# State-space stage: order of the decays, C times B over 128 partitions, and two moved VectorE steps

## The chip, the cores and the metric

The kernel runs on one core of a Trainium2 chip. The time is the device time of the whole program in microseconds (us), taken over several executions; the profile is one more execution, recorded by the hardware profiler. The core has TensorE (PE; its weight loads are listed as PEld), VectorE (DVE), ScalarE (ACT), GpSimd (POOL) and the queue engine SyncE (SP), which work side by side and wait for one another by semaphores.

## The reference, cut to what matters

`x` has 2 sequences of 2048 tokens with 512 channels, all in float32. Three layers follow one another, each added to `x`: half a gated feed-forward layer (ternary weights, 2048 hidden), a state-space layer, and the same feed-forward layer again. The change is in the state-space layer:

```
z, x, B_toks, C_toks, dt_toks = split(u @ W_in.T)         # 512, 512, 64, 64, 8 columns
x, B, C = silu(causal depthwise conv of 4 taps (x, B, C) + conv_b)
dt = softplus(dt_toks + dt_bias);  dA = exp(dt * -exp(A_log))       # one per head, 8 heads of 64 channels
S = S * dA_t + dt_t * outer(x_t, B_t);   y_t = S @ C_t              # token by token, state 64 x 64 a head
y = (y + D_param * x) * silu(z);   out = y @ W_out.T
```

## The kernel before, in words

The scan is computed in chunks of 128 tokens. Inside a chunk the sum over earlier tokens becomes a masked product: C times B (128 by 128 tokens), times a matrix of decays for each head, times dt times x. What comes from earlier chunks enters through the state, scaled by the decay from the chunk's begin.

Four chunks (c = 0 to 3) make a group of 512 tokens of one sequence. There are 8 groups; the two sequences alternate. Six run in a loop; the seventh has `front` LAST and no `ahead`, and the eighth (LAST) has no `front`. While a group `g` goes through its chunks, the projections, the convolution and softplus of the next group (`front`) and the layer norm of the one behind it (`ahead`) are put between the steps of `g`. Every engine has its own program, written out by hand in one fixed order; nothing is reordered at run time but by waits on semaphores (`wait_ge`). `after(q)` is the count that a semaphore has after q chunks.

TensorE in a chunk (`group` of the block `tensor`) does, in this order:

- `chunk_decays` (L1904): waits for POOL's masked log-decays `am`; then `seg` (L1910, four float16 products of 128x512 with the whole array, the decays between tokens, 8 heads) and `turn` (L1918, four float16 products of 128x512 into halves of the array's columns, tile form 128*64, the decay from the chunk's begin).
- `chunk_start` (L1923): C times B (L1930) over the 64 partitions in which B and a copy of C lie, and the transpose of B (L1931). Both have the tile form 64*128.
- `project_out` of the chunk before (L1975; waits for `y4_done`, that is for `yv` times silu(z), and for `res_done`). For c = 0 it is instead the first convolution projection of `front`.
- `turn_x` (L1937, waits for ACT's `ecb`), further projections of `front` (L1850, L1885), `chunk_y` (L1949 and L1956; waits for `dtx`, `lx` and `cd`), again a projection of `front`, and `chunk_state` (L1966; waits for `y1_done` and `dtxe`).

In a profile's row the tile form stands after the names, as in 128*128 or 128*64.

VectorE in a chunk: `gm` (C times B masked, L1748), `btok` (L1750), `lx` times `gm` (L1753), `residual(g, c - 1)` (L1739, waits for `project_out`), `dtx` (L1763, waits for `turn_x`), then for c = 0 the taps of the convolution, for c = 1 `softplus_end(front, 0)` (9 small steps, L1711 to L1718, each waiting for the one before), for c = 2 `softplus_end(front, 1)` (L1722 to L1733), for c = 3 `normalize(ahead)` (L1661); then the pass over y (`y1`, L1777), for c = 1 `variance(ahead)` (L1652, L1655), the state's decay `s1` (L1783), `yv` times silu(z) (`y4`, L1791), the state's sum `s2` (L1795) and the taps of the next convolution block (L1680).

ScalarE makes `lx` (exp of `seg`, L1587) and then `ecb` (exp of `turn`, L1591). POOL makes `dx` (L1492), `cd` (L1496, waits for `ecb`), `dtxe` (L1501, waits for `dtx`), the four parts of `am` for the next chunk (L1476), and for c = 1 `rstd` of `ahead` (L1465). SP copies C of the next group onto both halves of the partitions (`move_c`, L1408, two transfers of 128 KB), and moves the chunks' rows.

Of the kernel before, what the change touches and what calls it, by code (L numbers as in the profile page):

```python
# [25 lines left out]
P = 128  # L26
B, L, D, E = 2, 2048, 512, 2048
H, N, HD = 8, 64, 64
# [17 lines left out]
def macaron_kernel(nc, u, w_up, w_gate, w_down, w_in, w_out, conv_w, conv_b, head_par, out):  # L46
    top = ExitStack()

    def sb(ctx, name, shape, dt=F32):
        return ctx.enter_context(nc.sbuf_tensor(name, shape, dt))  # L50
# [10 lines left out]
    with top:  # L61
# [43 lines left out]
        def after(n):  # L105


            return n + 1
# [1119 lines left out]
        def ssm_part():  # L1228
            ctx = ExitStack()
            with ctx:  # L1230
                xpad = sb(ctx, "s_xpad", [P, TAPS - 1 + TG])
                hist = sb(ctx, "s_hist", [P, B, NCONV, TAPS - 1])
                xc = sb(ctx, "s_xc", [P, B, NCONV, TG])
                cc = sb(ctx, "s_cc", [P, B, TG])
                zs = sb(ctx, "s_zs", [P, B, KD, TG])
                dtv = sb(ctx, "s_dtv", [P, CH * H])
                sp_t = sb(ctx, "s_sp", [P, 7, CH * H])
# [32 lines left out]


                mix = ps(ctx, "s_mix", [P, 2 * D])
                bc = mix[:, 0:P + N]
                y_ps = mix[:, D // 2:D // 2 + D].rearrange("p (k i) -> p k i", k=KD)
                st_ps = mix[:, 3 * D // 2:2 * D]
                out_ps = ps(ctx, "s_out", [P, D])
# [54 lines left out]
                done_before = ((stat_done, CH), (mv_done, 1), (var_done, 1), (rstd_done, 1), (xn_done, 1), (tr_done, KD),  # L1331
                               *((s, KD // 2) for s in wide_free))

                N_SET = 8


                W_TR, W_BC, W_DTA, W_ALL = (0, 1, 2, 3), 4, 5, 16
# [17 lines left out]
                def order(g):  # L1355
                    return 2 * g[0] + g[1]
# [32 lines left out]
                def half(r):  # L1389
                    return slice(r * N, (r + 1) * N)  # L1390
# [9 lines left out]
                with nc.Block() as block:  # L1400

                    @block.sync
                    def _(sp):
                        def move_c(f):
                            n = order(f)
                            sp.wait_ge(xc_done, after(NCONV * n + 1))
                            for r in range(2):
                                sp.dma_start(cc[half(r), f[1], :], xc[N:2 * N, f[1], 4, :]).then_inc(cc_in, 16)  # L1408

                        def load(f):  # L1410

                            sp.wait_ge(xn_done, after(order(f)))
                            sp.dma_start(xa[:, 2, :, :], out_v[:, bass.ds(tile(f, 0), CH), :]).then_inc(x_in, 16)

                        def load_chunk(f, c):
                            sp.dma_start(xa[:, 0, c, :], out_v[:, bass.ds(tile(f, c), 1), :]).then_inc(r_in, 16)

                        def store_chunk(g, c):
                            q = CH * order(g) + c
                            sp.wait_ge(res_done, after(q + 1))  # L1420
                            sp.dma_start(out_v[:, bass.ds(tile(g, c), 1), :], xa[:, 0, c, :]).then_inc(chunks_out, 16)

                        start_counts(sp, [], done_before)
                        load((0, 1))
                        for c in range(CH):
                            load_chunk(FIRST, c)
                        sp.wait_ge(rows_out, 16 * NG)
                        move_c(FIRST)

                        def group(g, front, ahead):  # L1430
                            if ahead is not None:
                                load(ahead)
                            if front is not None:
                                move_c(front)
                            for c in range(CH):
                                store_chunk(g, c)
                                if front is not None:
                                    sp.wait_ge(chunks_out, 16 * (CH * order(g) + c + 1))
                                    load_chunk(front, c)

                        all_groups(sp, group)
                        sp.wait_ge(cc_in, 32 * NG)

                    @block.gpsimd
                    def _(pool):
# [8 lines left out]
                        nc.gpsimd.memset(state[0], 0.0).then_inc(set_done, 1)  # L1454
                        nc.gpsimd.memset(state[1], 0.0).then_inc(set_done, 1)
                        nc.gpsimd.memset(tri[:, :], 1.0).then_inc(set_done, 1)
                        pool.wait_ge(set_done, 5)
                        mask(tri[:, :], tri[:, :], 0, 1, -1).then_inc(set_done, 1)
                        mask(tri16[:, :], ones16[:, :], 0, 1, -1).then_inc(set_done, 1)
                        mask(after16[:, :], ones16[:, :], -1, -1, 1).then_inc(set_done, 1)  # L1460
# [22 lines left out]
                        def group(g, front, ahead):  # L1483
                            b = g[1]
                            for c in range(CH):
                                q = CH * order(g) + c
                                if c == 0:
                                    pool.wait_ge(xc_done, after(NCONV * (order(g) + 1)))
                                    pool.wait_ge(cc_in, 32 * (order(g) + 1))
                                    taken(pool, g, w_dec(g))  # L1490
                                pool.wait_ge(y1_done, after(q))
                                nc.gpsimd.tensor_tensor(dx[:, :, :], xc[:, b, 0:KD, cols(c)], over(chan_d, P), ALU.mult)\  # L1492
                                  .then_inc(dx_done, 1)
                                pool.wait_ge(ecb_done, after(q + 1))
                                pool.wait_ge(y_done, after(q))
                                nc.gpsimd.tensor_tensor(cd[:, :, :], ecb[:, :, :],  # L1496
                                                        cc[:, b, cols(c)].unsqueeze(1).to_broadcast([P, H // 2, P]), ALU.mult)\
                                  .then_inc(cd_done, 1)
                                pool.wait_ge(dtx_done, after(q + 1))
                                pool.wait_ge(st_done, after(q))  # L1500
                                nc.gpsimd.tensor_tensor(heads(dtxe[:, :]), heads(dtx[:, :]), over(to_end(b, c), HD), ALU.mult)\  # L1501
                                  .then_inc(dtxe_done, 1)
                                if c < CH - 1:
                                    masked(g, c + 1)
                                elif front is not None:
                                    masked(front, 0)
                                if c == 1 and ahead is not None:
                                    inv_std(ahead)
# [130 lines left out]
                    def _(dve):  # L1639
# [102 lines left out]
                        def group(g, front, ahead):  # L1742
                            b = g[1]
                            for c in range(CH):
# [8 lines left out]
                                nc.vector.tensor_tensor(lx[:, :, :], lx[:, :, :],  # L1753
                                                        gm[:, :].unsqueeze(1).to_broadcast([P, H, P]), ALU.mult)\
                                  .then_inc(m_done, 1)
                                if c:
                                    residual(g, c - 1)
                                if c == 0:
                                    dve.wait_ge(a_done, after(order(g) + 1))
                                dve.wait_ge(xt_done, after(q + 1))  # L1760
# [2 lines left out]
                                nc.vector.tensor_tensor(heads(dtx[:, :]), heads(turn[:, :]), over(dt[:, b, c, :], HD),  # L1763
                                                        ALU.mult).then_inc(dtx_done, 1)

                                if c == 0 and front is not None:
                                    taps(front, 0)
                                if c in (1, 2) and front is not None:
                                    softplus_end(front, c - 1)
                                if c == (2 if ahead is BEHIND else 3) and ahead is not None:  # L1770
                                    normalize(ahead)
                                if c == 1 and ahead is not None:
# [4 lines left out]
                                nc.vector.tensor_tensor(yv[:, :, :], y_ps, dx[:, :, :], ALU.add).then_inc(y1_done, 1)  # L1777
                                if c == 1 and ahead is not None:
                                    variance(ahead)
                                if c == 0:  # L1780
                                    taken(dve, g, w_dec(g))
                                dve.wait_ge(s2_done, after(q))
# [44 lines left out]
                    def _(pe):  # L1827
# [76 lines left out]
                        def chunk_decays(g, c):  # L1904
                            q, b = CH * order(g) + c, g[1]
                            pe.wait_ge(am_done, after(q + 1))
                            pe.wait_ge(lx_done, after(q))
                            for r in range(2):
                                for part in range(2):
                                    last = nc.tensor.matmul(seg[:, r * 512:(r + 1) * 512], after16[:, :],  # L1910
                                                            am[:, part, 4 * r:4 * r + 4, :].rearrange("p h i -> p (h i)"),
                                                            start=(part == 0), stop=(part == 1))
                            last.then_inc(seg_done, 1)
                            pe.wait_ge(dtx_done, after(q))
                            pe.sem_inc(pe_free, 1)
                            for part in range(2):
                                for r in range(2):
                                    last = nc.tensor.matmul(turn[half(r), :], ones16[:, 0:N],  # L1918
                                                            am[:, part, 4 * r:4 * r + 4, :].rearrange("p h i -> p (h i)"),
                                                            start=(part == 0), stop=(part == 1), skip_group_check=True)  # L1920
                            last.then_inc(cb_done, 1)

                        def chunk_start(g, c):  # L1923
                            q, b = CH * order(g) + c, g[1]
                            if c == 0:
                                pe.wait_ge(xc_done, after(NCONV * (order(g) + 1)))
                                pe.wait_ge(cc_in, 32 * (order(g) + 1))
                            pe.wait_ge(y1_done, after(q))
                            pe.sem_inc(pe_free, 1)
                            nc.tensor.matmul(bc[:, 0:P], xc[0:N, b, 4, cols(c)], cc[0:N, b, cols(c)], start=True, stop=True)  # L1930
                            nc.tensor.transpose(bc[:, P:P + N], xc[0:N, b, 4, cols(c)], ident[0:N, 0:N]).then_inc(bc_done, 1)  # L1931

                        def turn_x(g, c):
                            q, b = CH * order(g) + c, g[1]
# [149 lines left out]
```

## Time and profile before

| | |
|---|---|
| time, median of 3 runs | 1843.69 us (1842.53 to 1843.81) |
| profiled execution | 1840.33 us, its span 1838.6 us |
| granted TensorE clock | 1.00 of full speed throughout |
| busy | PE 96%, PEld 69%, DVE 75%, ACT 50%, POOL 45% |
| state-space stage | about 654 us to 1235 us of the span |
| one group in the loop | 71.04 us |

Busy is the time in which an engine had an instruction in hand. A timeline row gives the start of an instruction or of a run of equal ones, its duration, and in brackets the idle time ahead of it with what ended it. The ends of PE's matmuls are modelled, so what one run of matmuls really took is read from its start to the start of the next.

### The profile page before, as it was taken

The numbers are of one execution on the slowest core, as the hardware profiler recorded it, in microseconds if no ns is written. First come the engines' busy times: TensorE is split into PE (matmuls) and PEld (weight loads), VectorE is DVE, ScalarE is ACT, GpSimd is POOL, SyncE is SP. The second block draws the span as 40 slices with busy tenths as digits, with TensorE's granted clock in tenths as the row PEclk, the third lists the DMA queues.
The fourth block names the chain that finished last, engine by engine and source line by source line (L and its number), as shares of the span: only waits on it lengthen the run. The fifth ranks groups of instructions, "written<-read, shape, count | busy, mean of one in ns | idle before, by whom it ended". The sixth has DMA issues, their size and how long they took to land. (4 is left out here: it accounts for less than half of the span.)

```text
span 1838.6 us, 35155 instructions
## 1 busy us (share of the span) xinstructions
PE 1766.3 (96%) x13078; PEld 1262.9 (69%) x13078; DVE 1375.5 (75%) x2311; ACT 912.7 (50%) x1372; POOL 822.6 (45%) x554
## 2 busy tenths in 40 slices
PE   4899999999999999999999999889999999999998
PEld 2364888888888844444444444454888888888887
DVE  6948787778865758697697696757777777877755
ACT  6314456465473555435444444424465474574653
POOL 0496454262443515454454454545253352443533
PEclk9999999999999999999999999999999999999999
DMA  7032121311214031111111111110221202112100
GB/s 320 1 93 40 47 41 46 86 36 50 40 46 138 0 98 29 52 35 52 58 40 52 57 34 35 58 62 18 78 41 46 63 28 80 40 46 63 40 23 23
DMA packets 132329, 102.79 MB, mean 56 GB/s; under 512 B 100752, under 2 KB 100752, under 8 KB 130448
## 3 DMA queue, kind: packets, MB, share of 16 engines
q1 hardware_dynamic: 132240, 101.77, 18.5%
q8 instruction: 36, 0.59, 0.1%
q14 instruction: 53, 0.43, 0.1%
HBM read 49.59 MB, written 25.17 MB: 41 GB/s over the span
## 5 line engine op out<-in xcount | busy, mean ns | idle before, releaser
L445 POOL TENSOR_TENSOR f_hlo<-f_h,f_hhi 128x768 f16<-128x768 f32 x135 | 201.6, 1494 | 613.4 <-ACT f_hhi L595 584.8
L1042 PE MATMUL f_down_ps<-wd,f_hhi 128*128 128x256 fp8e4 x1440 | 318.4, 272 | 3.1 <-DVE xa L799 3.1
L1042 PE MATMUL f_down_ps<-wd,f_hlo 128*128 128x256 fp8e4 x1440 | 318.5, 273 | 0.0
L1116 PE MATMUL f_gate_ps<-spare 128*128 128x256 f16 x2496 | 306.1, 272 | 0.0
L1116 PEld LDWEIGHTS f_gate_ps<-spare 128*128 128x128 fp8e4 x2496 | 236.6, 97 | 40.8
L1116 PE MATMUL f_up_ps<-spare,wu 128*128 128x256 f16 x1664 | 213.5, 273 | 0.1
L799 DVE SCALAR_TENSOR_TENSOR xa<-f_down_ps,out_scale,xa 128x512 f32<-128x512 f32 x195 | 136.4, 744 | 59.8 <-PE f_down_ps L1042 59.5
L1116 PEld LDWEIGHTS f_up_ps<-spare,wu 128*128 128x128 fp8e4 x1664 | 160.7, 98 | 21.4 <-issue 0.4
L1042 PEld LDWEIGHTS f_down_ps<-wd,f_hhi 128*128 128x128 f16 x1440 | 140.9, 98 | 21.3 <-issue 4.9
L1042 PEld LDWEIGHTS f_down_ps<-wd,f_hlo 128*128 128x128 f16 x1440 | 140.9, 98 | 16.2
L1850 PE MATMUL s_wide<-xnt,late 128*128 128x512 f32 x320 | 145.4, 597 | 4.1 <-issue 2.1
L1476 POOL TENSOR_TENSOR s_am<-s_tri,s_al 128x512 f16<-128x512 f16 x128 | 145.9, 1169 | 6.1 <-DVE s_al L1733 6.1
L445 POOL TENSOR_TENSOR f_hlo<-late,f_hhi 128x1024 f16<-128x1024 f32 x68 | 148.5, 2184 | 0.0
L1680 DVE SCALAR_TENSOR_TENSOR s_xc<-s_xpad,late,s_xc 128x512 f32<-128x512 f32 x120 | 121.5, 1013 | 19.1 <-ACT s_xc L1542 16.3
L880 DVE SCALAR_TENSOR_TENSOR f_h<-f_h,hid_scale,f_tr_ps 128x512 f32<-128x512 f32 x104 | 77.4, 745 | 69.3 <-ACT f_h L635 69.3
L1975 PE MATMUL s_out<-late,s_yv 128*128 128x512 f32 x256 | 117.7, 602 | 0.0
L445 POOL TENSOR_TENSOR f_hlo<-spare,f_hhi 128x1024 f16<-128x1024 f32 x52 | 110.8, 2130 | 0.0
L874 DVE TENSOR_TENSOR f_tr_ps<-f_gate_ps,spare 128x512 f32<-128x512 f32 x104 | 72.8, 700 | 50.0 <-PE f_gate_ps L1116 50.0
L1116 PE MATMUL f_tr_ps<-spare 128*128 128x256 f16 x832 | 107.8, 273 | 0.3 <-DVE late L773 0.2
L630 ACT ACTIVATE f_h<-f_up_ps,silu_scale 128x512 f32<-128x512 f32 x104 | 71.4, 687 | 73.5 <-PE f_up_ps L1116 73.5
L1116 PE MATMUL f_gate_ps<-spare,wg 128*128 128x256 f16 x832 | 107.8, 273 | 0.0
L595 ACT ACTIVATE f_hhi<-f_h 128x768 f16<-128x768 f32 x120 | 97.1, 810 | 20.9 <-DVE f_h L887 19.1
(223 smaller groups left out, 3332.2 us busy)
## 6 DMA issues: line engine op xcount, KB each, us to landing
res<-xa SPq DMA_DIRECT2D x16, 1024.0 KB, 4.3
xa<-res SPq DMA_DIRECT2D x16, 1024.0 KB, 5.4
xa<-in_u SPq DMA_DIRECT2D x8, 1024.0 KB, 5.4
xa<-res SPq DMA_DIRECT2D x32, 256.0 KB, 2.6
res<-xa SPq DMA_DIRECT2D x32, 256.0 KB, 2.0
spare<-in_w_up SPq DMA_DIRECT2D x4, 1024.0 KB, 10.7
late<-in_w_gate SPq DMA_DIRECT2D x4, 1024.0 KB, 18.0
late<-in_w_in SPq DMA_DIRECT2D x1, 2320.0 KB, 8.8
```

The source lines that it names most:

```text
L445: last = nc.gpsimd.tensor_tensor(hlo[:, p, a:b, :], src, hhi[:, p, a:b, :], ALU.subtract)
L595: nc.scalar.activation(hhi[:, p, 0:n, :], h[:, p % 2, 0:n, :], ACT.Copy).then_inc(hhi_done, 1)
L630: nc.scalar.activation(h[:, p % 2, 0:2, :], two(A_ps[p % 2][:, :]), ACT.Silu, scale=silu_scale[:, 0:1]).then_inc(sil_done, 1)
L799: nc.vector.scalar_tensor_tensor(dst, src, out_scale[:, 0:1], dst, ALU.mult, ALU.add)\
L874: nc.vector.tensor_tensor(G_ps[:, :], C_ps[:, :], p5_sb, ALU.add).then_inc(c22_done, 1)
L880: nc.vector.scalar_tensor_tensor(at, at, hid_scale[:, 0:1], two(G_ps[:, :]), ALU.mult, ALU.mult)\
L1042: last = nc.tensor.matmul(at, part[:, p, kind, m * P:(m + 1) * P], wd[:, weight, p, :], start=(p == 0 and part is hhi and (m == 0 or name ...
L1116: last = nc.tensor.matmul(acc[:, j * HT:(j + 1) * HT], w[:, k, e * P:(e + 1) * P], xop[part][:, o, k, :, :], start=(fresh and (j, k, part) ...
L1476: last = nc.gpsimd.tensor_tensor(am[:, part, 4 * r:4 * r + 4, :], tri16[:, :].unsqueeze(1).to_broadcast([P, H // 2, P]), al[:, g[1], part, ...
L1680: nc.vector.scalar_tensor_tensor(xc[:, b, blk, :], xpad[:, t:t + TG], cvw[:, blk, t:t + 1], xc[:, b, blk, :], ALU.mult, ALU.add).then_inc( ...
L1850: last = nc.tensor.matmul(acc[:, :], win[:, k, row:row + P], xnt[:, k, :], start=(k == 0), stop=(k == KD - 1))
L1975: last = nc.tensor.matmul(out_ps[:, :], yv[:, k, :], wout[:, k, :], start=(k == 0), stop=(k == KD - 1))
```

## The change

- C times B is computed over all 128 partitions. A new tile `cz`, a part of `spare`, holds C in its lower 64 partitions and zeros in the upper 64; POOL clears it once at the begin of the stage, and `move_c` sends a third transfer for each group. The transpose of B goes over 128 partitions too and gives 128 columns, of which the same 64 are used.
- In `chunk_decays`, `turn` is computed first and `seg` second. The wait for `lx_done` goes with `seg`.
- `softplus_end(front, 0)` is moved from ahead of `y1` to behind `variance(ahead)`, ahead of `s1` and `y4`.
- `residual(g, c - 1)` is moved from ahead of `dtx` to behind it.

```diff
+                cz = spare[:, 4096:4096 + B * TG].rearrange("p (b t) -> p b t", b=B)
-                bc = mix[:, 0:P + N]
+                bc = mix[:, 0:2 * P]
-                N_SET = 8
+                N_SET = 9
@@ SP, move_c
-                            for r in range(2):
-                                sp.dma_start(cc[half(r), f[1], :], xc[N:2 * N, f[1], 4, :]).then_inc(cc_in, 16)
+                            for dst in (cz[half(0), f[1], :], cc[half(0), f[1], :], cc[half(1), f[1], :]):
+                                sp.dma_start(dst, xc[N:2 * N, f[1], 4, :]).then_inc(cc_in, 16)
@@ SP, before move_c(FIRST)
+                        sp.wait_ge(set_done, N_SET)
@@ POOL, at the begin
+                        nc.gpsimd.memset(cz, 0.0).then_inc(set_done, 1)
-                        pool.wait_ge(set_done, 5)
+                        pool.wait_ge(set_done, 6)
@@ DVE, group
-                                if c:
-                                    residual(g, c - 1)
...
                                 nc.vector.tensor_tensor(heads(dtx[:, :]), heads(turn[:, :]), over(dt[:, b, c, :], HD),
                                                         ALU.mult).then_inc(dtx_done, 1)
+                                if c:
+                                    residual(g, c - 1)
                                 if c == 0 and front is not None:
                                     taps(front, 0)
-                                if c in (1, 2) and front is not None:
-                                    softplus_end(front, c - 1)
+                                if c == 2 and front is not None:
+                                    softplus_end(front, 1)
...
                                 nc.vector.tensor_tensor(yv[:, :, :], y_ps, dx[:, :, :], ALU.add).then_inc(y1_done, 1)
                                 if c == 1 and ahead is not None:
                                     variance(ahead)
+                                if c == 1 and front is not None:
+                                    softplus_end(front, 0)
@@ PE, chunk_decays
                             pe.wait_ge(am_done, after(q + 1))
-                            pe.wait_ge(lx_done, after(q))
-                            (seg: four products, seg_done)
                             pe.wait_ge(dtx_done, after(q))
                             (turn: four products, cb_done)
+                            pe.wait_ge(lx_done, after(q))
+                            (seg: four products, seg_done)
@@ PE, chunk_start
-                            nc.tensor.matmul(bc[:, 0:P], xc[0:N, b, 4, cols(c)], cc[0:N, b, cols(c)], start=True, stop=True)
-                            nc.tensor.transpose(bc[:, P:P + N], xc[0:N, b, 4, cols(c)], ident[0:N, 0:N]).then_inc(bc_done, 1)
+                            nc.tensor.matmul(bc[:, 0:P], xc[:, b, 4, cols(c)], cz[:, b, cols(c)], start=True, stop=True)
+                            nc.tensor.transpose(bc[:, P:2 * P], xc[:, b, 4, cols(c)], ident[:, :]).then_inc(bc_done, 1)
```

All waits on `cc_in` count 48 for a group in place of 32.

## Rows read from the trace of the kernel before

**Rows 1.** The page, part 1: busy time, share and instructions of each engine.
```profile
PE 1766.3 (96%) x13078; PEld 1262.9 (69%) x13078; DVE 1375.5 (75%) x2311; ACT 912.7 (50%) x1372; POOL 822.6 (45%) x554
```
**Rows 2.** Busy time in the six loop groups (PE, PEld, DVE, ACT, POOL; then clock).
```profile
689.84:1116.83 426.99, 413.05 (x2053) 195.63 (x2052) 336.93 (x512) 196.09 (x314) 207.30 (x175) 1.00 0.14 45
```
**Rows 3.** PE's waits in the loop groups (us in total, times, longest).
```profile
PE s_mix L1966 <- DVE s_yv L1777: 7.9, 6, 1.3
PE s_mix L1949 <- issue: 2.2, 6, 0.4
PE s_wide L1850 <- issue: 1.8, 6, 0.3
PE s_seg L1910 <- POOL s_am L1476: 1.5, 6, 0.3
```
**Rows 4.** PE's waits in the seventh and eighth group.
```profile
PE s_mix L1949 <- DVE s_dtx L1763: 3.7, 3, 1.4
PE s_mix L1966 <- DVE s_yv L1777: 2.4, 3, 1.1
```
**Rows 5.** PE's timeline from a chunk's state to the next chunk's turn_x, no wait.
```profile
951.45 0.65 PE L1966 MATMUL s_mix<-s_dtxe,late 128*64 128x256 f32 x4
952.03 1.04 PE L1910 MATMUL s_seg<-s_am,s_after 128*128 128x512 f16 x4
953.00 0.62 PE L1918 MATMUL s_turn<-s_am,late 128*64 128x512 f16 x4
953.55 0.48 PE L1930 MATMUL s_mix<-s_cc,s_xc 64*128 64x128 f32 x2
953.88 0.22 PE L1931 MATMUL s_mix<-ident,s_xc 64*128 64x64 f32 x1
954.02 3.70 PE L1975 MATMUL s_out<-late,s_yv 128*128 128x512 f32 x8
957.56 0.60 PE L1937 MATMUL s_turn<-ident,s_xc 128*128 128x128 f32 x4
```
**Rows 6.** PE's timeline, the same product between neighbours of its own tile form.
```profile
900.26 3.60 PE L1975 MATMUL s_out<-late,s_yv 128*128 128x512 f32 x8
903.69 1.04 PE L1840 MATMUL s_wide<-ident,xn 128*128 128x128 f32 x8
904.57 1.03 PE L1910 MATMUL s_seg<-s_am,s_after 128*128 128x512 f16 x4
```
**Rows 7.** PE's products of y and of the state in chunk 1 of a loop group, timeline.
```profile
929.47 1.09 PE L1949 MATMUL s_mix<-s_lx,s_dtx 128*64 128x128 f32 x16 [0.37 <-issue]
930.50 0.67 PE L1956 MATMUL s_mix<-s_cd,late 64*64 64x128 f32 x16
936.12 0.65 PE L1966 MATMUL s_mix<-s_dtxe,late 128*64 128x256 f32 x4 [1.32 <-DVE s_yv L1777]
```
**Rows 8.** DVE's timeline in chunk 1 of the same group.
```profile
928.09 0.68 DVE L1739 TENSOR_TENSOR xa<-xa,s_out 128x512 f32<-128x512 f32 x1
928.69 0.68 DVE L1763 TENSOR_TENSOR s_dtx<-s_turn,s_dt 128x512 f32<-128x512 f32 x1
929.29 0.17 DVE L1711 TENSOR_SCALAR s_sp<-s_dtv 128x32 f32<-128x32 f32 x1
935.28 0.69 DVE L1777 TENSOR_TENSOR s_yv<-s_mix,s_dx 128x512 f32<-128x512 f32 x1 [0.30 <-DVE s_sp L1718]
936.70 0.69 DVE L1791 TENSOR_TENSOR s_yv<-s_yv,s_zs 128x512 f32<-128x512 f32 x1
```
**Rows 9.** DVE's timeline before the loop, POOL idle: first step of softplus and first behind nine.
```profile
671.30 0.18 DVE L1711 TENSOR_SCALAR s_sp<-s_dtv 128x32 f32<-128x32 f32 x1
673.46 0.65 DVE L1722 SCALAR_TENSOR_TENSOR s_sp<-s_sp 128x32 f32<-128x32 f32 x3
```
**Rows 10.** POOL's timeline in chunk 1 and at the begin of chunk 2.
```profile
930.45 4.03 POOL L1476 TENSOR_TENSOR s_am<-s_tri,s_al 128x512 f16<-128x512 f16 x4
936.54 1.11 POOL L1465 TENSOR_TENSOR s_rstd<-s_var,neg_half 128x4 f32<-128x4 f32 x1 [2.06 <-DVE s_var L1655]
```

More of the change, by code:

```diff
@@ L1441, in _ @@
                         all_groups(sp, group)
-                        sp.wait_ge(cc_in, 32 * NG)
+                        sp.wait_ge(cc_in, 48 * NG)
                     @block.gpsimd
@@ L1488, in group @@
                                     pool.wait_ge(xc_done, after(NCONV * (order(g) + 1)))
-                                    pool.wait_ge(cc_in, 32 * (order(g) + 1))
+                                    pool.wait_ge(cc_in, 48 * (order(g) + 1))
                                     taken(pool, g, w_dec(g))
@@ L1906, in chunk_decays @@
                             pe.wait_ge(am_done, after(q + 1))
-                            pe.wait_ge(lx_done, after(q))
[L1908 to L1913, printed above, removed]
                             pe.wait_ge(dtx_done, after(q))
@@ L1921, in chunk_decays @@
                             last.then_inc(cb_done, 1)
+                            pe.wait_ge(lx_done, after(q))
+                            for r in range(2):
+                                for part in range(2):
+                                    last = nc.tensor.matmul(seg[:, r * 512:(r + 1) * 512], after16[:, :],
+                                                            am[:, part, 4 * r:4 * r + 4, :].rearrange("p h i -> p (h i)"),
+                                                            start=(part == 0), stop=(part == 1))
+                            last.then_inc(seg_done, 1)
                         def chunk_start(g, c):
@@ L1926, in chunk_start @@
                                 pe.wait_ge(xc_done, after(NCONV * (order(g) + 1)))
-                                pe.wait_ge(cc_in, 32 * (order(g) + 1))
+                                pe.wait_ge(cc_in, 48 * (order(g) + 1))
                             pe.wait_ge(y1_done, after(q))
                             pe.sem_inc(pe_free, 1)
-                            nc.tensor.matmul(bc[:, 0:P], xc[0:N, b, 4, cols(c)], cc[0:N, b, cols(c)], start=True, stop=True)
-                            nc.tensor.transpose(bc[:, P:P + N], xc[0:N, b, 4, cols(c)], ident[0:N, 0:N]).then_inc(bc_done, 1)
+                            nc.tensor.matmul(bc[:, 0:P], xc[:, b, 4, cols(c)], cz[:, b, cols(c)], start=True, stop=True)
+                            nc.tensor.transpose(bc[:, P:2 * P], xc[:, b, 4, cols(c)], ident[:, :]).then_inc(bc_done, 1)
                         def turn_x(g, c):
```

## The prediction

> **What bounds the kernel now.** I read the page's busy times first, then busy time by stretch over the state-space stage, PE's waits there, and last the timelines of one group, engine by engine. The page shows PE busy for 96% of the span [rows 1], and in the six loop groups for 413 of 427 us, DVE for 337, at a granted clock of 1.00 [rows 2]. Each loop group repeats the same pattern, so one group is enough. PE is the bound; a change gains what it takes from PE's own time or from PE's few waits. Those are, per loop group, 1.32 us for the pass over y ahead of the state product, 0.37 us ahead of L1949 and 0.25 us for POOL's am [rows 3]. The row of L1949 names "issue", but DVE's dtx ends at 928.69 + 0.68 = 929.37 and the product starts at 929.47 [rows 7, 8]: it is a wait for dtx. All three lie in chunk 1. A fourth, 0.3 us ahead of L1850, lies in chunk 0. In the last two groups, where fewer projections stand between the steps, the first two waits sum to 6.1 us [rows 4].
>
> PE's busy time also holds something else. Project_out takes 3.43 us from start to start between neighbours of its own tile form [rows 6], and 3.54 us behind the 64*128 form [rows 5]. Seg should take 4 x 512 columns at 2.4 GHz, 0.85 us, and takes 0.97 ahead of turn; turn, which fills both column halves at once, should take 0.43 and takes 0.55 [rows 5]. So a change of tile form costs about 0.1 us on the side that is left and, for float32, 0.11 us on the side that is entered (0.02 for float16).
>
> **C over zeros and the order of the decays.** From the state product to project_out the form now changes four times: 128*64, 128*128, 128*64, 64*128, 128*128 [rows 5]. After the change it is 128*64 (state, turn), then 128*128 to the end: once. The stretch from L1966 to L1937 takes 957.56 - 951.45 = 6.11 us. New sum: state 0.48 (0.58 without the change behind it), turn 0.43 + 0.10, seg 0.87, C times B 2 x 0.11, the wider transpose 0.11, project_out 3.43, together 5.64: 0.47 us gained. The 0.11 for a 128-column float32 product with the whole array is the spacing of eight transposes, (904.57 - 903.69)/8 [rows 6]; C times B has no row in this form. Its price lies between 0.11 and the 0.16 that L1930's two instructions take now, so the gain lies between 0.36 and 0.47 a chunk. I take 0.47, since 512 columns over the whole array take 3.43/8 = 0.43, four times 0.11.
>
> In chunk 1 PE waits for am anyway, so the state's share is hidden: 0.37. In chunk 0 transposes of form 128*128 stand on both sides of the decays, so turn is framed by two changes either way, and what C times B saves is hidden, since the next projection waits 0.3 us for ACT's copies [rows 3]: 0 gained. The Trainium skill, "TensorEngine Tiling (Array Packing)", Theoretical Speedup, speaks against this edit: it gives a contraction of 64 rows up to twice the speed in row tiles. By it C times B would lose up to its own 0.22 us in 32 chunks, 7 us. L1930 has only one tile to run, whose two instructions take 0.33 us [rows 5], so by the rows nothing is lost.
>
> Seg ends 1.88 us behind the state's start in place of 1.55. ACT's table load for exp runs ahead of lx, lx and ecb take 1.6 us, and turn_x comes 3.8 us behind seg's end: covered in chunks 1 to 3. In chunk 0 ACT is held by its copies until 907.9, after seg is done in both orders.
>
> **Residual behind dtx.** In chunk 1 DVE is behind, not waiting: residual at 928.09 and dtx at 928.69 have no idle time ahead of them. With dtx first it ends at 928.77, and L1949 starts at 928.87 instead of 929.47 [rows 7, 8]: 0.60 us gained, of which PE's shorter stretch is 0.37. Residual's 0.60 falls into the time in which DVE waits for the y products or is hidden behind POOL-bound softplus steps (chunk 2). What waits for res_done (the next project_out and the store) is some 10 us off.
>
> **Softplus behind y1.** Y1 no longer waits for nine steps. The y products end 1.7 us behind L1949's start (930.50 + 0.67 - 929.47), so y1 starts at 930.6, and the state product no longer waits: 1.32 us gained [rows 7]. With 0.60 this is 1.92 by the state product of chunk 1. Now y4 is late, and project_out of chunk 2 waits for it. Today y4 ends 936.70 + 0.69 - 935.28 = 2.11 us behind y1's start [rows 8]; now it ends at 930.64 + 2.11 + S = 932.75 + S, with S the time of the nine steps. PE is ready for project_out at 934.2 + 0.48 + 0.53 + 0.87 + 0.33 = 936.4, so the stall is S - 3.6 (above 0).
>
> S is 5.99 us today (929.29 to 935.28), while POOL's dtxe and am run [rows 8, 10], and 2.16 us with POOL idle [rows 9]. POOL's am is four instructions of 1.0 us, and beside it the steps end one at a time, each with one of them. At the new place, from 931.7, am still runs to about 933.9 (0.6 earlier than now): two steps held, 2.2 us; seven free ones at 0.24 make 1.7; and dx, started behind rstd, holds one for up to 1.0. S lies between 3.9 and 4.9; I take 4.7, so 1.05 us of stall. The bounds are 2.16 (no stall) and 5.99 (2.4).
>
> **Third transfer, memset, wait for set_done.** SP issues 0.6 us more for each group; C is needed over 30 us later. The memset of 128x1024 takes about 1 us at 655 us, and PE first asks for set_done at 675: 0, and if the cover went, 1 us once. The waits on cc_in are met long before.
>
> **Sum.** Loop group: 1.92 + 0.47 (chunk 2) - 1.05 + 0.47 (chunk 3) = 1.81; six make 10.9. In the seventh group DVE is busy nearly without a break from chunk 1 on, so the gain there is what DVE's chain loses: dtx 0.6 earlier, S shorter by 1.0, residual given back ahead of softplus' second part 0.3 to 0.6, a stretch of 0.47 less some DVE wait: 1.2. In the eighth: 0.47, 0.37 and 0.37 from stretches and 0.3 from am, which follows the earlier dtx: 1.5; chunk 0 waits for ACT either way. Together 13.6 us. The profiled execution goes from 1840.3 to 1826.7. The median of the runs lies 3.4 above it, so the measured time goes from 1843.7 to 1830.
>
> **Rivals.**
> (a) The steps stay held. POOL goes am, rstd, dx without a break from 929 to 936, so S stays near 5.99 and y4 ends at 938.7, where project_out starts today (938.69). Then only 0 to 0.3 is left at chunk 2 and 0.47 of chunk 3: 0.6 a group, 3.6 + 2 = 5.6 us, 1838. For it: am held every step; against it: rstd held nothing (936.54 to 937.65, with y4 at 936.70 taking its plain 0.69 beside it) [rows 8, 10]. The Trainium skill, "SBUF — State Buffer", Who interferes with whom, says that a VectorE instruction with two SBUF inputs and a GpSimd one that reads SBUF block each other for the whole instruction, which would make rstd count. By the row y4 beside rstd contradicts it for this one instruction.
> (b) The changes of form are not what costs the 0.1 us, or the product over zeros takes it back: the stretches give nothing. Left are the two waits: 0.37 + 1.32 - about 0.9 = 0.8 a group, 5 us + 2, 1837. Against it: the starts in rows 5 and 6.
> (c) No stall at all: S under 3.6: 1.05 x 6 = 6.3 more, 1824.
> (d) Slower. Y4 behind softplus becomes the bound: if all nine steps, s1 and y4 are held by POOL at 1.0 to 1.5 us each, y4 ends at 931.7 + 9.0 + 1.0 + 1.5 = 943.2, project_out comes 4.5 us later than today, DVE's taps behind it push the next lx, dtx and y1 by as much; 0.5 is regained: 4 us a group, 24 - 2, 1866. It decides once y4 ends later than about 939.4 in this group's time, S above 6.6. Against it: POOL has nothing to run between dx, done at 936, and cd, which waits for ecb at about 937.7.
>
> **Chances.** Forecast, gain 10 to 17 us: 0.58. (a) 0.16, (b) 0.07, (c) 0.08. (d) in any size, with an unforeseen wait: 0.06, and 0.05 for a gain or loss inside 0.2% (3.7 us, about what a measurement of this kernel tells from no change). So faster 0.89, same 0.05, slower 0.06. The range goes from no stall (1824) to (a) and a little beyond (1839).
>
> **What would show it.** L1910 behind L1918 on PE, with 6.1 us from L1966 to L1937 down to 5.6 in chunk 3; no wait of L1966 for y1 and none of L1949 in chunk 1 beyond 0.2; a new wait of L1975 in chunk 2 for L1791, about 1 us, six times; the nine steps in 4 to 5 us; the loop group 69.2 us in place of 71.04. I am wrong if L1930 and L1931 take over 0.5 us, if the state product in chunk 2 waits for y1 (there the margin is about 0.1 us), or if the new wait is over 2.4 us.

## The result and the profile after

The changed kernel takes 1825.43 us (median of 4 runs, 1824.01 to 1827.68); before it was 1843.75 us (4 runs). The ratio is 0.9903, with a 95% interval of 0.9886 to 0.9920: 15 to 21 us faster. The forecast was 1830 us in a range of 1824 to 1839. So the direction and the pattern held; the gain forecast, 13.6 us, was too small. The profiled executions are 1840.33 us before, faster than all four runs, and 1827.68 us after, the slowest of the four, so the traces are compared stage by stage and not by their whole spans.

The traces say where the gain is. The state-space stage is measured from its first convolution projection to the start of the last project_out. It goes from 654.02 to 1229.22 before, 575.2 us, and from 656.26 to 1215.27 after, 559.0 us: 16.2 us less. A loop group takes 68.9 us, from one group's first transposes to the next's (PE's timeline of the changed kernel; start, duration, engine, line, operation):

```profile
899.47 1.04 PE L1846 MATMUL s_wide<-ident,xn 128*128 128x128 f32 x8
968.36 1.04 PE L1846 MATMUL s_wide<-ident,xn 128*128 128x128 f32 x8
```

That is 68.89 in place of 71.04. In chunk 3 no wait stands in the stretch that answers to [rows 5]:

```profile
945.52 0.65 PE L1972 MATMUL s_mix<-s_dtxe,late 128*64 128x256 f32 x4
946.01 0.60 PE L1917 MATMUL s_turn<-s_am,late 128*64 128x512 f16 x4
946.54 1.04 PE L1924 MATMUL s_seg<-s_am,s_after 128*128 128x512 f16 x4
947.42 0.38 PE L1936 MATMUL s_mix<-spare,s_xc 128*128 128x128 f32 x2
947.64 0.27 PE L1937 MATMUL s_mix<-ident,s_xc 128*128 128x128 f32 x1
947.75 3.60 PE L1981 MATMUL s_out<-late,s_yv 128*128 128x512 f32 x8
951.18 0.60 PE L1943 MATMUL s_turn<-ident,s_xc 128*128 128x128 f32 x4
```

Read it from start to start: state 0.49, turn 0.53, seg 0.88, C times B 0.22, the transpose 0.11, project_out 3.43. The stretch takes 5.66 us in place of 6.11. (A row's own duration, such as 0.27 us for the transpose, is longer than what it adds, since the ends are modelled.)

Four of PE's waits over the whole stage (us in total, times, longest) answer to [rows 3, 4]. Those of L1955 (it was L1949) and L1972 (it was L1966) are gone from the loop groups; what is left of them (3.3 us here, and 2.4 us in two waits of L1972) lies in the seventh and eighth group. In their place L1981, project_out, waits for y4:

```profile
PE s_out L1981 <- DVE s_yv L1797: 3.6, 7, 0.5
PE s_mix L1955 <- DVE s_dtx L1765: 3.3, 3, 1.7
PE s_wide L1856 <- ACT xnt L1526: 3.1, 7, 0.5
PE s_turn L1917 <- POOL s_am L1480: 2.7, 8, 0.3
```

DVE's timeline in chunk 1, as in [rows 8], shows softplus' nine steps at their new place, between the pass over y and s1, y4:

```profile
926.43 0.69 DVE L1781 TENSOR_TENSOR s_yv<-s_mix,s_dx 128x512 f32<-128x512 f32 x1 [1.32 <-issue]
927.57 0.17 DVE L1715 TENSOR_SCALAR s_sp<-s_dtv 128x32 f32<-128x32 f32 x1
927.77 0.90 DVE L1716 TENSOR_SCALAR s_sp<-s_sp 128x32 f32<-128x32 f32 x1
928.71 0.35 DVE L1717 RECIPROCAL s_sp<-s_sp 128x32 f32<-128x32 f32 x1
929.09 0.58 DVE L1718 TENSOR_TENSOR s_sp<-s_sp 128x32 f32<-128x32 f32 x1
929.71 0.19 DVE L1719 TENSOR_TENSOR s_sp<-s_sp 128x32 f32<-128x32 f32 x1
929.94 0.18 DVE L1720 TENSOR_SCALAR s_sp<-s_sp 128x32 f32<-128x32 f32 x1
930.15 1.50 DVE L1722 SCALAR_TENSOR_TENSOR s_sp<-s_sp 128x32 f32<-128x32 f32 x3
931.69 0.43 DVE L1789 TENSOR_TENSOR late<-late,s_dec 128x256 f32<-128x256 f32 x1
932.03 0.68 DVE L1797 TENSOR_TENSOR s_yv<-s_yv,s_zs 128x512 f32<-128x512 f32 x1
```

Beside it POOL runs:

```profile
925.59 4.04 POOL L1480 TENSOR_TENSOR s_am<-s_tri,s_al 128x512 f16<-128x512 f16 x4
929.59 1.00 POOL L1469 TENSOR_TENSOR s_rstd<-s_var,neg_half 128x4 f32<-128x4 f32 x1
930.57 1.04 POOL L1496 TENSOR_TENSOR s_dx<-s_xc,late 128x512 f32<-128x512 f32 x1
```

The steps take 931.69 - 927.57 = 4.12 us. A step is "held" when it takes longer than with POOL idle, where these take about 0.2 us each and the reciprocal 0.35. Three are held: one ends at 928.67 and one at 929.67, each with a part of am (about 1.0 us a part), and one of the last three with dx, which ends at 931.61. The two that run beside rstd (929.59 to 930.59) take their plain 0.19 and 0.18.

### The profile page after: what moved, and what is told of

Same layout as the page of the kernel before. It is cut to its first block and busy times, and to the rows that moved or that the text cites. A ratio compares the mean times of both kernels' runs of the same rounds, so it can differ in the third digit from the quotient of the medians.

```text
span 1825.9 us, 35144 instructions
## 1 busy us (share of the span) xinstructions
PE 1760.0 (96%) x13078; PEld 1267.5 (69%) x13078; DVE 1355.2 (74%) x2311; ACT 913.2 (50%) x1372; POOL 818.4 (45%) x555
## 5 line engine op out<-in xcount | busy, mean ns | idle before, releaser
L1684 DVE SCALAR_TENSOR_TENSOR s_xc<-s_xpad,late,s_xc 128x512 f32<-128x512 f32 x120 | 115.5, 963 | 19.2 <-ACT s_xc L1546 16.3
L1981 PE MATMUL s_out<-late,s_yv 128*128 128x512 f32 x256 | 116.0, 596 | 3.6 <-DVE s_yv L1797 3.6
L1013 PE MATMUL f_up_ps<-xnt,wu 128*128 128x512 f16 x384 | 94.3, 390 | 14.7 <-DVE f_h L787 8.6
```

The costliest lines, as they stand in the source:

```text
L1013: last = nc.tensor.matmul(acc[:, :], w[:, k, e * P:(e + 1) * P], part[:, k], start=(k == 0 and part is xhi), stop=(k == KD - 1 and part is ...
L1684: nc.vector.scalar_tensor_tensor(xc[:, b, blk, :], xpad[:, t:t + TG], cvw[:, blk, t:t + 1], xc[:, b, blk, :], ALU.mult, ALU.add).then_inc( ...
L1981: last = nc.tensor.matmul(out_ps[:, :], yv[:, k, :], wout[:, k, :], start=(k == 0), stop=(k == KD - 1))
```

## The experiments

Each is compared with runs of the kernel before that were taken beside it; "stage" is measured as above, 575.2 us before and 559.0 after, "group" the loop group, 71.04 and 68.89.

**e1_order and e2_zeros: each edit of TensorE alone.** e1: `turn` ahead of `seg`. e2: `cz`, its memset and the third transfer, the product and the transpose over 128 partitions.

```
e1  chunk_decays:  turn products, cb_done;  then wait lx_done, seg products, seg_done
e2  matmul(bc[:, 0:P], xc[:, b, 4, cols(c)], cz[:, b, cols(c)]);  transpose(bc[:, P:2 * P], ..., ident[:, :])
```

> The kernel before with turn computed ahead of seg, and nothing else. Theory (each change of the tile form costs about 0.1 us on the side left, and 0.11 us for float32 or 0.02 us for float16 on the side entered): three changes in place of four, the stretch from the state product to turn_x in chunk 3 takes 5.99 us in place of 6.11; over the stage 1 to 2 us less, too little for the clock to tell. Rival (the forms cost nothing and it is the product over zeros alone that is faster): 6.11 us and no change.

> The kernel before with C times B and the transpose over 128 partitions, seg still first. Theory: the forms go 128*64, 128*128, 128*64, 128*128, three changes: the stretch in chunk 3 takes 5.97 us in place of 6.11. Rival (the product over zeros is what is faster): the whole gain of the two edits shows here, about 5.65 us.

**e3_forms: both together**, VectorE's order as before.

> Both edits of TensorE (turn first, C over zeros), VectorE's order as before. Theory: one change of form in place of four, so the stretch in chunk 3 takes 5.65 us, 0.46 less, more than the 0.12 and 0.14 of each edit alone. In chunk 1 nothing is gained, since dtx and y1 come from VectorE when they did: the gain there goes into the two waits (0.37 and 1.32 us, the first about 0.7 now). 0.9 us a loop group, 5.5 to 7 us in all. Rival (the edits add up): 5.85 us in chunk 3, 3 to 4 us in all.

The same stretch of chunk 3, its first and last row, in e1, e2 and e3:

```profile
952.45 0.65 PE L1966 MATMUL s_mix<-s_dtxe,late 128*64 128x256 f32 x4
958.45 0.60 PE L1937 MATMUL s_turn<-ident,s_xc 128*128 128x128 f32 x4
```
```profile
950.36 0.65 PE L1970 MATMUL s_mix<-s_dtxe,late 128*64 128x256 f32 x4
956.33 0.60 PE L1941 MATMUL s_turn<-ident,s_xc 128*128 128x128 f32 x4
```
```profile
948.07 0.65 PE L1970 MATMUL s_mix<-s_dtxe,late 128*64 128x256 f32 x4
953.72 0.60 PE L1941 MATMUL s_turn<-ident,s_xc 128*128 128x128 f32 x4
```

6.00, 5.97 and 5.65 us, against 6.11. The two edits alone give 0.11 and 0.14, together 0.46. That is what counting changes of form gives (three, three and one in place of four) and what neither the product over zeros nor the order explains by itself. Groups: 70.76, 70.78, 70.09; stages 572.9, 573.2, 567.9; ratios 0.9983 (0.9974 to 0.9993), 0.9984 (0.9975 to 0.9994) and 0.9946 (0.9930 to 0.9963). No run separates the change of form itself from the weight load that goes with it. E3's stage gain, 7.3 us, is a little over the 5.5 to 7 expected. Chunk 1 gives nothing, as expected; L1953 there waits longer for dtx:

```profile
926.55 1.09 PE L1953 MATMUL s_mix<-s_lx,s_dtx 128*64 128x128 f32 x16 [0.62 <-DVE s_dtx L1767]
933.19 0.65 PE L1970 MATMUL s_mix<-s_dtxe,late 128*64 128x256 f32 x4 [1.32 <-DVE s_yv L1781]
```

**e7_transpose_form: two changes of form put back** into the changed kernel.

```diff
-   nc.tensor.transpose(bc[:, P:2 * P], xc[:, b, 4, cols(c)], ident[:, :])
+   nc.tensor.transpose(bc[:, P:P + N], xc[0:N, b, 4, cols(c)], ident[0:N, 0:N])
```

> The changed kernel with the transpose of B back in the form 64*128 (64 columns), between two steps of form 128*128. Theory: two changes of form come back, 0.36 us in the stretch of chunk 3 (6.01 us against 5.66) though the transpose itself has half the columns; 0.7 us a loop group, since in chunk 2 the wait for y4 takes it; 4 to 6 us slower than the changed kernel. Rival (the forms cost nothing): 5.6 us and no change.

```profile
946.10 0.65 PE L1972 MATMUL s_mix<-s_dtxe,late 128*64 128x256 f32 x4
948.30 0.27 PE L1937 MATMUL s_mix<-ident,s_xc 64*128 64x64 f32 x1
952.04 0.60 PE L1943 MATMUL s_turn<-ident,s_xc 128*128 128x128 f32 x4
```

The stretch takes 5.94 us, 0.28 more, with half the columns in the transpose. Group 69.63, stage 564.8, ratio to before 0.9933 (0.9916 to 0.9949); its median, 1831.3, lies 5.9 us above the changed kernel's. Only the size in the stretch was off, by 0.07 us: the two changes cost 0.28 there, not 0.36.

**e5_resid and e6_softplus: each edit of VectorE alone**, and **e4_schedule: both**, TensorE as before.

```
e5  lx *= gm;  dtx;  residual(g, c - 1);  ...
e6  y1;  variance(ahead);  softplus_end(front, 0);  s1;  y4;  ...      (c == 1)
```

> The kernel before with residual behind dtx alone. Theory: L1949 in chunk 1 starts 0.37 us earlier, but softplus' nine steps start when they did (residual now stands ahead of them), so y1 ends when it did and the state product waits 0.37 us longer: no gain, within 1 us. Rival (the edits are independent): 0.37 us a group stays, 2.6 us in all.

> The kernel before with the first part of softplus behind y1 alone. Theory: the state product's wait of 1.32 us in chunk 1 goes, project_out of chunk 2 waits about 0.1 us for y4; 1.2 us a loop group, 7 to 9 us in all. The nine steps take 4.0 to 4.4 us there in place of 5.99. Rival (softplus stays held at its new place, 5.5 to 6 us): a wait of 1.5 us or more, no gain.

> Both edits of VectorE (residual behind dtx, softplus' first part behind y1), TensorE's order and forms as before. Theory: 0.37 us at L1949 and 1.32 us at the state product gained in chunk 1, a stall of 0.1 to 0.3 us at project_out of chunk 2: 1.5 us a loop group, 10 to 11 us in all. Rival (the moved softplus costs what it gives): a stall of 1 us or more in chunk 2, 5 us or less in all.

| | group | stage | ratio to before |
|---|---|---|---|
| e5, residual | 70.67 | 571.7 | 0.9979 (0.9969 to 0.9988) |
| e6, softplus | 69.99 | 568.9 | 0.9962 (0.9948 to 0.9976) |
| e4, both | 69.85 | 566.6 | 0.9954 (0.9940 to 0.9968) |

The theory fell in e5 and its rival held: 0.37 us a group stays, 3.5 us over the stage. Measured from turn_x's start the steps do start when they did (4.22 us behind it in both), but POOL's dtxe and am follow dtx, which is 0.6 us earlier, and the held steps end with am. DVE and POOL in e5, chunk 1:

```profile
926.99 0.68 DVE L1761 TENSOR_TENSOR s_dtx<-s_turn,s_dt 128x512 f32<-128x512 f32 x1
928.19 0.65 DVE L1711 TENSOR_SCALAR s_sp<-s_dtv 128x32 f32<-128x32 f32 x1
932.86 0.65 DVE L1718 SCALAR_TENSOR_TENSOR s_sp<-s_sp 128x32 f32<-128x32 f32 x3
933.80 0.69 DVE L1777 TENSOR_TENSOR s_yv<-s_mix,s_dx 128x512 f32<-128x512 f32 x1 [0.30 <-DVE s_sp L1718]
```
```profile
928.75 4.03 POOL L1476 TENSOR_TENSOR s_am<-s_tri,s_al 128x512 f16<-128x512 f16 x4
```

Am ends at 932.78, and the last three steps, 0.65 us in all, run free behind it. E6 has the pattern expected, but less of it: the state product's wait is gone from the loop groups, the nine steps take 4.13 us, and project_out waits 0.27 us and not 0.1, so that a group gives 1.05 us in place of 1.2 and the stage 6.3 in place of 7 to 9. E4 gave less than expected, 1.19 us a group: its wait at project_out was 0.6 us, not 0.1 to 0.3. That is also less than e5 and e6 added up (1.42), since what residual gives makes TensorE wait longer for y4. E4's and e3's gains (8.6 and 7.3) add up to 15.9 us, the changed kernel's is 16.2: the two pairs hardly touch each other.

**e11_am_later: are the steps held by POOL?** One wait added to the kernel before, on POOL:

```diff
+   if c == 1 and front is not None:
+       pool.wait_ge(y1_done, after(q + 1))
    if c < CH - 1:
        masked(g, c + 1)
```

> The kernel before, where in chunk 1 POOL waits for y1 before it computes am for chunk 2. Nothing on VectorE is changed. Theory (the nine steps of softplus are held by POOL's instructions): the nine steps ahead of y1 take 3 to 3.5 us in place of 5.99 (dtxe still holds one), y1 starts at 932.3 in that group's time; TensorE then waits for am in chunk 2, so the time as a whole is within 1% of before. Rival (the steps are slow because each waits for the one before by semaphore): 5.9 to 6 us.

DVE, from the first of the nine steps to y1:

```profile
941.40 0.17 DVE L1713 TENSOR_SCALAR s_sp<-s_dtv 128x32 f32<-128x32 f32 x1
941.61 1.04 DVE L1714 TENSOR_SCALAR s_sp<-s_sp 128x32 f32<-128x32 f32 x1
943.07 0.19 DVE L1716 TENSOR_TENSOR s_sp<-s_sp 128x32 f32<-128x32 f32 x1
944.67 0.69 DVE L1779 TENSOR_TENSOR s_yv<-s_mix,s_dx 128x512 f32<-128x512 f32 x1 [0.30 <-DVE s_sp L1720]
```

3.27 us in place of 5.99, with every step still waiting for the one before: it is POOL that holds them. The time as a whole was missed: 1872 us in a single run, 1.5% above before and not within 1%. Why is under the last heading.

**e8_y4_first: softplus' first part behind y4.**

```diff
-   if c == 1 and front is not None: softplus_end(front, 0)      (ahead of s1, y4)
+   if c == 1 and front is not None: softplus_end(front, 0)      (behind y4, ahead of s2)
```

> The changed kernel with the first part of softplus one step later, behind y4 and ahead of s2. Theory (project_out of chunk 2 waits for y4 and for nothing else): its wait of 0.52 us goes in seven groups, 3 to 3.6 us less than the changed kernel. Rival: VectorE as a whole is late by then, so that the wait appears again at the y product or the state product of chunk 2: no gain.

The rival held. The wait is gone from project_out and stands, as 0.60 us, at the state product of chunk 2:

```profile
943.28 0.65 PE L1972 MATMUL s_mix<-s_dtxe,late 128*64 128x256 f32 x4 [0.60 <-DVE s_yv L1781]
```

Group 68.90, stage 559.5, ratio 0.9908 (0.9891 to 0.9924): no gain over the changed kernel.

**e9_both_y4: both parts behind y4. e10_both_y4_turn: and in chunk 0 turn behind the second transposes.**

```diff
-   if c == 2 and front is not None: softplus_end(front, 1)      (ahead of y1)
+   if c in (1, 2) and front is not None: softplus_end(front, c - 1)      (behind y4)
    e10, TensorE, c == 0: transposes(0, 2); seg; transposes(2, 4); turn; chunk_start
```

> The changed kernel with both parts of softplus behind y4 (chunk 1 and chunk 2). In e8 the wait of 0.52 us only moved, to the state product of chunk 2, which waits 0.60 us for y1, held there behind softplus' second part. Theory: with that part behind y4 too, no y1 and no y4 is late; the loop group takes 68.3 us in place of 68.9, the seventh group about 1 us less; 3.5 to 5 us less than the changed kernel. A third wait is possible where TensorE needs the decays' sums in chunk 3 (a_done), but they are ready about 4 us ahead. Rival (VectorE is full: each wait taken away appears one step later): 68.9 us again.

> As e9, and in chunk 0 turn is computed behind the second pair of transposes and not ahead of seg, so that it fills the 0.45 us in which TensorE waits for ScalarE's copies. Theory: that wait falls below 0.1 us, 0.4 us a group in seven groups, 2.5 to 3 us less than e9. Rival (ScalarE's copies or POOL's am set chunk 0 as a whole): no change.

PE's waits in the loop groups of e10, from 690 us on:

```profile
PE s_turn L1915 <- POOL s_am L1480: 2.1, 6, 0.3
PE s_wide L1844 <- ACT xnt L1526: 0.7, 1, 0.7
PE s_wide L1844 <- ACT s_zs L1563: 0.3, 1, 0.3
```

E9: group 68.25, stage 555.6, ratio 0.9895 (0.9878 to 0.9911). E10: group 67.66, stage 552.2, 1819.98 us, ratio 0.9873 (0.9857 to 0.9890). For the loop groups both theories held: 0.65 us less a group, then 0.59. In all, e9 gave less than expected. Its stage is 3.4 us shorter than the changed kernel's, just short of the 3.5 to 5, and its median only 1.3 us lower, within the intervals. The seventh group didn't give its 1 us: there the waits do fall, from 5.05 to 4.21 us, but one of them, for dtx, grows from 1.67 to 2.66 us, and the granted clock is 0.84 from 1140 to 1150 us behind it; the last two groups take 109.6 us in place of 109.2. By the stage e10 is 6.8 us shorter than the changed kernel; its median lies 5.5 us below, with intervals of the ratios that just overlap.

**e12_same: the kernel before again**, only a comment added.

> The kernel before once more, with nothing changed but a comment. In every comparison so far the medians differ by about 2 us more than the state-space stage does in the traces. If that lies in how the kernel before was built or run, this copy comes out 2 us faster than it as well; if it is scatter of the other stages, 0 with an interval that holds 0.

The ratio is 1.0003 (0.9993 to 1.0013), so it is scatter, not how the kernel was built. Its trace shows where the scatter came from in this execution: its stage takes 576.9 us, 1.7 more than that of the execution profiled before, as told under the last heading.

## Why the prediction was right

**The forms.** Each piece of the stretch was forecast within 0.01 us, their sum as 5.64 against 5.66. That 128 columns over the whole array cost 0.11 each was right, so rival (b) is out. The loss of up to 7 us that the prediction set against leaving the row tiles didn't come either: C times B and the transpose take 947.75 - 947.42 = 0.33 us, where they took 954.02 - 953.55 = 0.47. Chunk 0 takes 915.36 - 899.47 = 15.89 us to the next chunk's decays, before 15.85: the 0 that was forecast.

**The two waits of chunk 1.** From the decays to the state product it was 936.12 - 919.54 = 16.58 us, it is 929.86 - 915.36 = 14.50: 2.08 gained, forecast 1.92, with 0.08 more than forecast on either side of the y products' start. By the runs alone, softplus' move takes away the whole wait of the state product (e6) and residual's gives 0.37 us (e5); neither needs the other.

**The term that was mis-sized: S.** I took 4.7 us for the nine steps out of bounds of 3.9 to 4.9, and a stall of 1.05; it is 4.12 and about 0.5:

```profile
929.86 0.65 PE L1972 MATMUL s_mix<-s_dtxe,late 128*64 128x256 f32 x4
932.77 3.70 PE L1981 MATMUL s_out<-late,s_yv 128*128 128x512 f32 x8 [0.52 <-DVE s_yv L1797]
936.31 0.60 PE L1943 MATMUL s_turn<-ident,s_xc 128*128 128x128 f32 x4
```

The stretch takes 6.45 us with its wait, 0.34 more than before; forecast was 0.58 more. Y4 ends 6.28 us behind y1's start, which fits 2.11 + 4.12 = 6.23. The prediction let two steps pass while am still ran, and seven behind it at 0.24 each. Four passed, in 929.71 - 927.57 = 2.14 us: the first was not held (0.17 us), near the border between two parts of am, and the reciprocal took the 0.35 us that it takes with POOL idle, as it does beside am before, in e5 and in e6. The smaller S is worth 0.24 us a group, the waits of chunk 1 another 0.16: per group -0.04 + 2.08 - 0.34 + 0.45 = 2.15 in place of 1.81, 2.0 us over six. The seventh and eighth group gave 112.39 - 109.15 = 3.2 us, forecast 2.7. Together 16.2 against 13.6.

**The rivals.** (a) needed S near 5.99; the steps are held by am and dx but not by rstd, as y4 was not in the rows of before. (c) needed S under 3.6. None of the prediction's signs of being wrong came: L1936 and L1937 take 0.33 us, the state product of chunk 2 doesn't wait, and the new wait is 0.52 us. (d) asked for a y4 later than TensorE can hide; e8 and e9 show how near such a bound is: each step of VectorE taken out of one wait stood in the next until both parts were moved. The rule of the Trainium skill on the shared port that the prediction quotes ("SBUF — State Buffer", Who interferes with whom) is borne out by the steps with two SBUF inputs that end with parts of am and with dx, and not by rstd, whose 128x4 elements are listed with 1.00 us on POOL while a step with two SBUF inputs passes beside it in 0.19. Why rstd doesn't hold them is not shown.

**What is left between 16.2 and the 17.9 us of the ratio** lies outside what was forecast, and within the interval. It can't be read from the two profiled executions as wholes: they differ by 12.7 us only, because the changed kernel's took 2.2 us more ahead of the stage (it begins at 656.26 and not at 654.02) and 1.3 us more behind it, where both kernels do the same. The last section has what the traces show of it.

## What to carry to other kernels

Where TensorE is the bound and its row shows busy without gaps, read from start to start and sort the same product by its neighbours: a change of tile form showed as 0.1 us on either side, and two edits that each save one change saved three together. A small step on VectorE can cost what POOL is doing beside it (here 0.2 us free and up to 1.0 beside a part of am), so place it by POOL's timeline and behind whatever TensorE waits for. Ask of each wait taken away which one stands behind it: of the two further moves of softplus, the first alone gained nothing (e8), and both together took 0.65 us off a group (e9).

## What the runs showed of the hardware

TensorE's clock. In e11 PE waits 3.2 us for am in each loop group. In the group shown, the granted clock behind it falls to its lower level, 1.2 GHz, for some 7 us (busy time by stretch; the clock is the first number behind the five engines):

```profile
947.00:950.60 3.60, 0.49 (x4) 0.04 (x2) 3.56 (x4) 1.82 (x2) 3.60 (x4) 1.00 0.00 0
950.60:953.00 2.40, 2.32 (x8) 0.55 (x8) 1.32 (x2) 0.69 (x1) 2.40 (x3) 0.59 0.00 0
953.00:956.00 3.00, 3.00 (x8) 1.55 (x7) 1.87 (x3) 2.82 (x4) 1.31 (x2) 0.50 0.00 0
956.00:959.00 3.00, 3.00 (x6) 1.27 (x5) 0.33 (x1) 0.00 (x0) 0.00 (x0) 0.69 0.00 0
```

The decays, C times B and project_out then take 959.44 - 950.68 = 8.76 us in place of 942.23 - 936.70 = 5.53. So this wait costs 3.2 us and another 3.2 by the clock; less the wait of 1.3 us for y1 that is gone, this is the 5.1 us by which that group is longer (76.15 in place of 71.04). The six loop groups take 455.3 us in place of 427.0, which is why e11 misses its time.

The clock also falls behind shorter waits, and not in every execution. E12 is the same program as before. In the eighth group, behind a wait of 1.47 us for ecb, its 32 products of L1881 take 5.30 us from start to start, before they took 3.67, behind the same wait of 1.47 us:

```profile
1182.26 0.69 PE L1937 MATMUL s_turn<-ident,s_xc 128*128 128x128 f32 x4 [1.47 <-ACT s_ecb L1591]
1182.75 5.37 PE L1881 MATMUL s_wide<-xnt,late 128*128 128x128 f32 x32
1188.05 1.09 PE L1949 MATMUL s_mix<-s_lx,s_dtx 128*64 128x128 f32 x16
```

Its clock is 0.91 from 1180 to 1200 us, where the execution profiled before had 1.00. At the begin of the second feed-forward layer, behind 2.2 us of wait in all three, e12 and the changed kernel show 0.95 and 0.93 from 1215 to 1240 us, before 1.00. In the first feed-forward layer, whose program is the same in all, the changed kernel's execution shows 0.51 from 20 to 30 us, before and e12 1.00; 16 products of L1013 take 4.40 us there in place of 3.46. The clock is 0.83 there from 90 to 100 us, before 1.00. That fits the 2.2 us by which its stage begins late; e9 and e10 begin theirs as late, with 0.91 from 20 to 100 us as in the changed kernel. The execution profiled before had none of these dips, which fits its being 3.4 us faster than the median. So its stage, 575.2 us, is on the short side: against e12's 576.9, in an execution near the median, the changed kernel's 559.0 is 17.9 us less, as much as the ratio says. That is one execution of each; how often either kernel has such dips, the single profiles don't settle.
